# Ten of the attention's row gathers issued one stage earlier, the sums cleared by ScalarE, and no zeros laid under the score products

## The reference, cut to what matters

```python
def _L0_gnn_ref(x, edge_index, W, att_src, att_dst, bias):
    h = jnp.einsum('nf,fhd->nhd', x, W)              # 8 heads of 32
    a_src = jnp.sum(h * att_src, axis=-1)
    a_dst = jnp.sum(h * att_dst, axis=-1)
    src, dst = edge_index[0], edge_index[1]
    e = jax.nn.leaky_relu(a_src[src] + a_dst[dst], NEG_SLOPE)
    e_max = jax.ops.segment_max(e, dst, num_segments=N)
    e_exp = jnp.exp(e - e_max[dst])
    denom = jax.ops.segment_sum(e_exp, dst, num_segments=N)
    alpha = e_exp / (denom[dst] + 1e-16)
    msg = h[src] * alpha[:, :, None]
    out = jax.ops.segment_sum(msg, dst, num_segments=N)
    return jax.nn.relu(out.reshape(N, -1) + bias)
```

## Time and profile before

| | before |
|---|---|
| median of 3 runs | 3957.91 us (3952.92 to 3958.33) |
| the profiled execution | 3953.78 us, span 3952.0 us |
| busy: PE, DVE, ACT, POOL | 3103.2, 1812.7, 862.1, 2068.5 us |
| node score stage | 117.5 to 135 us of the span |
| attention stage | 135 to 1365 us of the span |
| mean granted clock of TensorE | 0.859 of full |

### The profile page before, as it was taken

One profiled execution on the slowest core, in us unless ns is written; L12 is line 12 of the kernel. 1 busy time (PEld: TensorE's weight loads), 2 busy tenths in 40 slices (PEclk: granted clock), 3 DMA queues, 4 the chain that ended last, 5 costly groups with the idle time before them and its releaser, 6 DMA issues. The chain is left out here.

```text
span 3952.0 us, 54002 instructions
## 1 busy us (share of the span) xinstructions
PE 3103.2 (79%) x13452; PEld 2313.1 (59%) x13453; DVE 1812.7 (46%) x3476; ACT 862.1 (22%) x1462; POOL 2068.5 (52%) x2020
## 2 busy tenths in 40 slices
PE   5478788888888763999932899999999986549991
PEld 4255566666665553666622777888888844425550
DVE  4466666666666663111147344444445453311114
ACT  5100000000000031322201333232322234313330
POOL 0577777777666046222212777777777701432330
PEclk9678888888888855999966999999999997669995
DMA  4455554444434124222244555555555400332225
GB/s 147 131 159 147 157 145 144 143 143 137 130 114 124 59 69 180 88 77 86 76 150 135 157 156 156 150 156 150 155 148 147 119 6 21 116 116 83 84 85 206
DMA packets 313076, 489.09 MB, mean 124 GB/s; under 512 B 54845, under 2 KB 212862, under 8 KB 312702
## 3 DMA queue, kind: packets, MB, share of 16 engines
q0 software_dynamic: 95232, 263.59, 22.6%
q1 hardware_dynamic: 199308, 194.22, 15.7%
q10 hardware_dynamic: 18388, 29.78, 2.2%
HBM read 404.96 MB, written 82.42 MB: 123 GB/s over the span
## 5 line engine op out<-in xcount | busy, mean ns | idle before, releaser
L808 POOL DMA_INDIRECT room<-h_table,src_idx x784 | 861.9, 1099 | 303.2 <-issue 235.2
L1915 POOL DMA_INDIRECT em_msg<-xn_table,src_idx x784 | 775.7, 989 | 368.4 <-issue 238.5
L1031 PE MATMUL at_ps<-room,at_member 128*128 128x264 f32 x2336 | 673.2, 442 | 32.0 <-DVE at_member L822 17.7
L1031 PEld LDWEIGHTS at_ps<-room,at_member 128*128 128x128 f32 x2336 | 478.9, 214 | 166.9 <-DVE room L915 43.8
L1996 PE MATMUL em_psa<-em_msg,em_member 128*128 128x256 f32 x2336 | 520.3, 379 | 1.2 <-DVE acc L1946 1.2
L1996 PEld LDWEIGHTS em_psa<-em_msg,em_member 128*128 128x128 f32 x2336 | 443.8, 190 | 61.9 <-DVE acc L1946 1.6
L1989 PE MATMUL em_pse<-em_We,em_attr_t 128*128 128x256 f32 x1552 | 377.7, 399 | 54.2 <-DVE em_msg L1940 54.2
L1940 DVE TENSOR_TENSOR em_msg<-em_pse,em_msg 128x1024 f32<-128x1024 f32 x196 | 230.6, 1218 | 323.5 <-DMA em_msg<-xn_table,src_idx 323.4
L1989 PEld LDWEIGHTS em_pse<-em_We,em_attr_t 128*128 128x128 f32 x1552 | 302.3, 200 | 106.9 <-DVE em_msg L1940 64.7
L2042 ACT ACTIVATE em_msg<-em_msg 128x1024 f32<-128x1024 f32 x196 | 207.3, 1058 | 711.2 <-DVE em_msg L1940 704.0
L1689 POOL DMA_INDIRECT y_table<-room,m0e_dest x112 | 107.4, 959 | 336.0 <-DVE room L1710 325.3
(11 more groups left out here) (373 smaller groups left out, 3768.7 us busy)
## 6 DMA issues: line engine op xcount, KB each, us to landing
at_dst_row<-dst_flat SPq DMA_DIRECT2D x98, 512.0 KB, 5.0
em_attr<-in_edge_attr_dram SPq DMA_DIRECT2D x97, 512.0 KB
room<-x_sorted SPq DMA_DIRECT2D x57, 516.0 KB, 3.4
room<-h_table,src_idx POOLq DMA_INDIRECT x784
at_resets<-reset_flat SPq DMA_DIRECT2D x784, 8.0 KB
m0c_rows<-y_table ACTq DMA_DIRECT2D x7, 1792.0 KB, 8.1
em_msg<-xn_table,src_idx POOLq DMA_INDIRECT x784
m1c_rows<-y_table ACTq DMA_DIRECT2D x7, 1792.0 KB, 10.3
```

What stands on the lines that cost most here:

```text
L808: pool.indirect_dma_start(msg[:, s, j, :], None, mem.h_table[:, :], bass.IndirectOffsetOnAxis(ap=mem.src_idx[:, c:c + 1].bitcast(u32), axi ...
L1031: ins = nc.tensor.matmul(ps_a[:, which, 0:MSG], member[which][:, j, :], msg[:, s, c, :], start=(j == 0), stop=False)
L1915: pool.indirect_dma_start(msg[:, s, j, :], None, mem.xn_table[:, :], bass.IndirectOffsetOnAxis(ap=mem.src_idx[:, c:c + 1].bitcast(u32), ax ...
```

## The change

Four things are done.

1. The first ten gathers of step 0 move from the attention stage to GpSimd's part of the node score stage. The remaining six, and all later ones, stay. Their code is the new function `gather_rows`.
2. ScalarE clears `acc` in the node score stage, in seven activations of 7 tiles (128 x 1848) each that copy a broadcast zero. GpSimd's memset is gone.
3. `spread_scores` lays no zeros. The first tile of a block is taken out of the loop, and its first product carries `start=True`, with which the rest of the bank counts as empty for the products that follow. Further tiles are in a loop behind a condition, `count > 1`. Where a slot must be released, a product 8 columns wide does so.
4. `zeros` in the attention stage is 128 columns wide and no longer 384.

```diff
+AHEAD = 10
+def gather_rows(pool, mem, msg, landed, k, j):
+
+    c, s = k * SC + j, k % SLOTS
+    pool.indirect_dma_start(msg[:, s, j, :], None, mem.h_table[:, :],
+                            bass.IndirectOffsetOnAxis(ap=mem.src_idx[:, c:c + 1].bitcast(u32), axis=0)).then_inc(landed[s], 16)
...
         @block.gpsimd
         def _(pool):
-            pool.memset(mem.acc[:, :, :], 0.0).then_inc(cleared, 1)
-            pool.wait_ge(cleared, 1)
+            for j in range(AHEAD):
+                gather_rows(pool, mem, msg, landed, 0, j)
+
+        @block.scalar
+        def _(act):
+            for t in range(0, NT, RT):
+                nc.scalar.activation(mem.acc[:, t:t + RT, :].rearrange("p t f -> p (t f)"),
+                                     mem.zeros[:, 0:1].to_broadcast([P, RT * MSG]), ACT.Copy).then_inc(cleared, 1)
+            act.wait_ge(cleared, NR)
...
-        zeros = sb("zeros", [P, CB * PT], bf16)
+        zeros = sb("zeros", [P, P], bf16)
...
         @block.gpsimd
         def _(pool):
             for k in range(NS):
-                s = k % SLOTS
                 if k >= SLOTS:
                     pool.wait_ge(slot_read, k - SLOTS + 1)
-                for j in range(SC):
-                    c = k * SC + j
-                    pool.indirect_dma_start(msg[:, s, j, :], None, mem.h_table[:, :],
-                                            bass.IndirectOffsetOnAxis(ap=mem.src_idx[:, c:c + 1].bitcast(u32), axis=0))\
-                        .then_inc(landed[s], 16)
+                for j in range(AHEAD if k == 0 else 0, SC):
+                    gather_rows(pool, mem, msg, landed, k, j)
...
                     if p == 0:
                         pe.wait_ge(taken, k)
-                    ins = nc.tensor.matmul(ps_s[:, p, 0:CB * PT], zeros[:, 0:P], zeros[:, :],
-                                           start=True, stop=False, skip_group_check=True)
-                    if p == 0 and free is not None:
-                        ins.then_inc(free, 1)
+                        if free is not None:
+                            nc.tensor.matmul(ps_s[:, 0, 0:HEADS], zeros[:, :], zeros[:, 0:HEADS],
+                                             start=True, stop=True, skip_group_check=True).then_inc(free, 1)
                     first, count, before = pairs_loop(pe, mem, b)
-                    with pe.Fori(0, count) as r:
-                        q, t = before + r, tile_of(first, r)
+
+                    def tile(q, t, begins):
                         pe.wait_ge(marked, q + 1)
                         for j in range(CB):
                             ins = nc.tensor.matmul(ps_s[:, p, j * PT:(j + 1) * PT], member_t[:, bass.ds(pair_slot(q) + j * P, P)],
-                                                   tile_at(mem.parts, t), start=False, stop=True, skip_group_check=True)
+                                                   tile_at(mem.parts, t), start=(begins and j == 0), stop=True, skip_group_check=True)
                         ins.then_inc(spread, 1)
+                    tile(before, first, True)
+                    with pe.If(count > 1):
+                        with pe.Fori(1, count) as r:
+                            tile(before + r, tile_of(first, r), False)
```

More of the change, by code:

```diff
@@ L581, in last_plus, with phase_node_scores @@
     return not isinstance(b, int) or b + n < NB
-def phase_node_scores(nc, mem):
+def gather_rows(pool, mem, msg, landed, k, j):
+    c, s = k * SC + j, k % SLOTS
+    pool.indirect_dma_start(msg[:, s, j, :], None, mem.h_table[:, :],
+                            bass.IndirectOffsetOnAxis(ap=mem.src_idx[:, c:c + 1].bitcast(u32), axis=0)).then_inc(landed[s], 16)
+def phase_node_scores(nc, mem, msg, landed):
     with ExitStack() as ctx:
@@ L702, in _, with phase_attention @@
             general(pe, body)
-def phase_attention(nc, mem, acc):
+def phase_attention(nc, mem, acc, msg, landed):
     LEAD = 3
@@ L714, in phase_attention @@
         sem = lambda n: new_semaphore(nc, mem, ctx, f"at_{n}")
-        msg = mem.room[:, :].rearrange("p (s c f) -> p s c f", s=SLOTS, c=SC)
         member = [sb(f"member{k}", [P, CB, P]) for k in range(3)]
@@ L741, in phase_attention @@
         slot_read = sem("slot_read")
-        landed = [gather_semaphore(nc, mem, "at_landed" + str(s)) for s in range(SLOTS)]
         reset_in = [sem(f"reset_in{s}") for s in range(2)]
@@ L2255, in build @@
             phase_front(nc, mem, a)
-            phase_node_scores(nc, mem)
+            msg = mem.room[:, :].rearrange("p (s c f) -> p s c f", s=SLOTS, c=SC)
+            landed = [gather_semaphore(nc, mem, "at_landed" + str(s)) for s in range(SLOTS)]
+            phase_node_scores(nc, mem, msg, landed)
             early.close()
-            phase_attention(nc, mem, acc)
+            phase_attention(nc, mem, acc, msg, landed)
         clear_semaphores(nc, mem)
```

## The result

| | before | after |
|---|---|---|
| median of 4 runs | 3955.93 us (3952.92 to 3958.33) | 3920.01 us (3918.49 to 3924.55) |
| ratio | | 0.9911, 95% interval 0.9896 to 0.9926 |
| span of the profiled execution | 3952.0 us | 3917.3 us |
| mean granted clock of TensorE | 0.859 | 0.862 |

The kernel is faster by 36 us of its medians and 34.7 us of its spans. I had forecast 21 us, and a range that ended at 3927. The size is outside it, and so are both of its terms. Every ratio in this document compares the faster executions of the two kernels alone, so that it can differ from the ratio of their medians.

A forecast was written before the change was run, and what follows sets the result against it. GpSimd's gather queue was taken to bound the attention stage's first half, TensorE held by its sequencer the second. -17 - 4 = -21 us on 3953.8 gave 3932.8, adjusted to the runs' median 3936.9; forecast 3936, range 3927 to 3947.

The forecast's parts named there:

- The two terms of the sum: Attention stage: -17 us from the earlier gather queue, -4 us from TensorE's score products without zeros in the second half.
- The sign of a wrong prediction: Attention stage: step 23 less than 13 us earlier would show the gathers' part wrong.
- The stage without the memset: Node score stage: VectorE's copy falls from 7.00 to about 0.54 us; VectorE done at 128.3, GpSimd 129.9, ScalarE 129.8.
- Rival 1: Node score stage: VectorE's copy and three casts block GpSimd's gathers, adding 3.5 us; time 3940; chance 0.12.
- So the stage ends at about 130: Node score stage: ends near 130, not 134.69; other engines start 4.4 us earlier, the eleventh gather at 131.3 or little later.
- Rival 3: Barrier after the node score stage: waiting for ten transfers, or a slow first gather, limits queue gain to 10-12 us; chance 0.06.
- The whole 17 us is in: Attention stage, first half: from step 5 gathers bound again, so the full 17 us lead arrives and passes step 23.
- The first block lies in the shade of a full queue: TensorE's first block in a second-half step: at most the zero product's own 0.17 us is gained.
- Between +0.1 and -0.3 us for a second block: TensorE's second block of two or more tiles: price of dispatch, move and branches, with as many taken branches as before.
- My upper end for the gain: TensorE, second half: the full 0.33 us of both zero products saved, 25 x 0.66 = -16 us.
- rival 4: TensorE's longer program must be fetched, stalling second-half steps; +22 us, time 3980; chance 0.04.
- rival 5: Attention stage: gathers are not the bound, so the lead does nothing; only 4.4 and 4 us remain, 3949; chance 0.03.

The follow-up runs named there:

- `e4_peel_keep_zero`: Kernel before with the first tile taken out of the loop, a condition behind it, both wide zero products kept; 4529.19 us, ratio 0.9962 (0.9930 to 0.9994).
- `e3_narrow_zero`: Kernel before with both zero products 8 columns wide instead of 384, the loop over tiles kept; 4536.17 us, ratio 0.9962 (0.9923 to 1.0001).

## Why the prediction was wrong in size

Faster was right, and both mechanisms were there. The two terms of the sum were mis-sized in opposite directions, -17 for the gathers against -9.7 measured and -4 for TensorE against -26.5, and both measured values lie outside the ends that I gave them (-13 to -18.5 and -16 to +5). That the total is off by 15 us and not by TensorE's 22 is luck: the gathers' error of 7 goes the other way. The sign of a wrong prediction that I had named for the gathers' part, step 23 less than 13 us earlier, came true.

**The stage without the memset.** The copy was to come down to 0.54 and takes 0.51; an activation was to take 1.76 us and takes 1.65; VectorE was to be done at 128.3 and is at 128.5. These steps held. Rival 1 supposed the rule that a VectorE copy or cast in a 2-port mode blocks the descriptors that GpSimd writes (the Trainium skill, "SBUF — State Buffer", "A bandwidth-pool intuition that's wrong (but worth ruling out)"). Beside one copy and three casts the ten gathers took 13.55 us where 1.18 + 9 x 1.25 = 12.4 was their least: 1.1 us more, not the 3.5 of rival 1. The longest, 1.71 us, ran from 126.63 to 128.34 and had the cast of 127.55 beside it. So rival 1 is refuted as a price, but the rule itself is not tested: a cast of 784 numbers takes 0.97 us, and so does the TENSOR_TENSOR on as many that stands between the casts, so that no row shows the casts in such a mode.

**"So the stage ends at about 130."** This step failed first. It ended at 134.6. (By my own numbers the others would have started 4.7 us earlier, 134.7 - 130, and not the 4.4 that I went on with; they started 0.6 earlier.) I took 1.27 us from the stage's end to the next gather from a stage in which GpSimd had only a memset; after an early gather it is 3.12. Rival 3 named this wait, and I gave it 0.06 for want of a row that showed it. Together with a first gather 1.0 us later than I put it (118.54 against 117.50) and the 1.1 us of stretching, of which I had taken 0.8, the eleventh gather starts at 135.21 and not 131.3. That is a lead of 13.9 us for 17.8.

**"The whole 17 us is in."** It should have been 13.9 then, and is 9.7 at step 23. The starts of each slot's last gather show where the rest went: 13.4 us earlier in steps 0 to 2, 11.3 in step 3, 10.5 in step 4, 8.4 in step 5, and anything from 8.1 to 11.3 in steps 6 to 23. So 9.7 at step 23 is in part chance: another step would have given up to 1.6 us more or less. In the first six steps the 96 gathers take 104.2 us and took 98.3. Apart from the 1.2 us of step 0, the lengthened ones stand in steps 3 and 5: the sixteen of step 3 take 19.4 us and took 16.5, those of step 5 18.0 and 16.4. Two of step 3:

```profile
194.13 2.00 POOL L588 DMA_INDIRECT room<-h_table,src_idx  x1 [0.30 <-issue]
...
207.16 1.73 POOL L588 DMA_INDIRECT room<-h_table,src_idx  x1 [0.30 <-issue]
```

VectorE used to idle 1.4 to 3.2 us a step there for the slot, and no longer does. I counted the end of these waits as gain and not that VectorE's work then lies beside more of the gathers. That this is what lengthened them is argued from two traces; no run separates it. The waits came back from step 4 and 5 on, as forecast, and step 23 was to stand at 651.5 and stands at 658.7.

**"The first block lies in the shade of a full queue."** This step failed for first blocks of two tiles. The bound of -0.17 us supposed a sequencer that is ahead. Its own row spoke against it: 16 products in 0.91 us at 1241.65, and 0.56 when they are only executed. With the first tile out of the loop they do take 0.56, and the block gains 0.49. Where the first block has one tile its eight products take 0.36 us in both traces, and the step holds.

**"Between +0.1 and -0.3 us for a second block."** I priced one dispatch, a move and two branches by their lengths, and wrote that a block of two or more tiles keeps its taken branches. This is the step that cost most. For a block of one tile the price holds (-0.10 and +0.13 us in its pieces); a block of two gains 0.65, and 36 of the last 48 blocks are such. Which blocks have a second tile was to be read before. What counts where TensorE waits for its sequencer is how many operations go by, each some 0.1 us, the register operations as much as the branches. `e4_peel_keep_zero` shows the loop alone at -0.60 / -1.27, and `e3_narrow_zero` the product's width at 0. My upper end for the gain, 25 x 0.66 = 16 us, was worked out from the product's columns, that is from the one thing that costs nothing. The measured 23.8 lies outside it.

**The other rivals.** TensorE's longer program made no gap (rival 4): no stretch of a late step is longer than before. The gathers were the bound up to step 24 (against rival 5), 15 scores still wait for them. The second half also has a slightly higher granted clock, 0.90 against 0.88 of full over 690 us to the stage's end, and the remainder of its steps is 2.7 us shorter in all (26.5 - 23.8); no run separates the two.

**What stays open.** That 9.7 and 26.5 us add up in the total is shown by the two traces of one chip only; the totals of the others gave less than their stretches, by an amount that their scatter hides. Why the other chips take half a millisecond more for the same program isn't known. The cause of the lead's loss between step 2 and step 5 is argued.

## What to carry to other kernels

Where the timeline shows "issue" between products that wait for nothing, price an edit by the number of sequencer operations it takes out of that path, register operations included, and not by the columns or the branch. Taking the first turn out of a loop was worth 0.65 us here for each time that the loop would have turned twice, and nothing where it turned once: count the turns before pricing it. A barrier behind moved gathers opens late: ten gathers issued early made their queue 8 us earlier and the next block's start on all engines 5 us later than none, and an end of GpSimd's list that falls with the other engines' last work gives the same lead for less, as seven gathers did.

## What the runs showed of the hardware

- A block with row gathers in it was left 2.4 to 2.7 us after the last gather instruction in all eleven traces that have one, one without 0.45 us after the last work.
- A bf16 product of 128 x 8 takes 0.17 us and one of 128 x 384 takes 0.33, and the difference is not seen where the next product came 0.9 to 1 us later. Eight products whose addresses come from registers take 1.07 us one behind the other, 0.13 us each; when they are in the queue already, 16 take 0.56.
- TensorE's sequencer: register operation 32 to 36 ns, fused one 46 to 65, move 29, table load 300, branch 67 to 78 not taken and 208 taken, the starts of operations some 0.1 us apart.
- An activation that fills 128 x 1848 fp32 with a broadcast zero takes 11.53 / 7 = 1.65 us, 0.89 ns an element, the same as the slope read from the line of another shape.
